# A token tower on one NeuronCore: four value buffers, an early v of batch 4, an early first expert unit, and a new order of the opening

## The reference

```python
h = onehot(x) @ embeddings                          # a row gather
q, k, v = split(layernorm(h) @ w_qkv)               # 16 heads of 16
q = q * cos + rotate_half(q) * sin                  # k too
attn = softmax(q @ k.T * 16 ** -0.5)                # 256 x 256 per head
h = h + (attn @ v) @ w_proj
y = layernorm(h)
chosen = argmax(y @ gate_w.T)                       # one of 8 experts
out = h + y + (y @ expert_w[e].T) * onehot(chosen)  # summed over e
```

## Time and profile before

| | us |
|---|---|
| median of 3 runs (310.54 to 310.95) | 310.89 |
| the profiled execution | 310.0 |
| its span | 308.2 |
| TensorE busy | 283.4 (92%) |
| VectorE busy | 243.4 (79%) |
| ScalarE busy | 132.7 (43%) |
| GpSimd busy | 85.9 (28%) |
| mean granted TensorE clock | 0.983 |

### The profile page before, as it was taken

How to read it: one execution, slowest core, us unless ns; L and a number is a source line. 1 busy time by engine, 2 the same in 40 slices (tenths; PEclk the granted TensorE clock), 3 DMA queues, 4 the chain that set the end, 5 groups by cost and what they waited for, 6 DMA issues and landing times.

```text
span 308.2 us, 5639 instructions
## 1 busy us (share of the span) xinstructions
PE 283.4 (92%) x2063; PEld 203.1 (66%) x2063; DVE 243.4 (79%) x602; ACT 132.7 (43%) x271; POOL 85.9 (28%) x103
## 2 busy tenths in 40 slices
PE   2998799888879999999999999999999999999895
PEld 2775566656646776777767776777666666667674
DVE  8798569968987799887988698878898874656765
ACT  3166117748664534364426433453453444331000
POOL 5736305636265012431222033201200210210300
PEclk9999579999999999999999999999999999999999
DMA  4530410830930580039101940166010010000011
GB/s 117 182 149 17 160 45 6 167 49 14 161 47 5 95 120 2 0 93 147 17 2 36 147 60 2 36 116 94 2 37 1 4 36 2 1 12 26 0 36 34
DMA packets 10803, 17.55 MB, mean 57 GB/s; under 512 B 2024, under 2 KB 4883, under 8 KB 10648
## 3 DMA queue, kind: packets, MB, share of 16 engines
q1 hardware_dynamic: 9988, 16.62, 26.2%
q0 software_dynamic: 768, 0.55, 0.7%
q10 hardware_dynamic: 20, 0.02, 0.0%
HBM read 5.30 MB, written 2.10 MB: 24 GB/s over the span
## 4 chain that ended last, share of the span: by engine, by line
PE 64%; DVE 24%; ACT 5%; issue 3%; DMA 1%; POOL 0%; SPq 0%; DVEq 0%; ACTq 0%
PE e_bank L475 18%; PE f_bank L475 10%; PE o_bank L652 9%; DVE neg_max L1003 7%; PE t_pair L617 5%; DVE acc L1101 4%; PE s_pair L475 4%; PE s_pair L578 3%; PE m_bank L475 3%; PE s_pair L481 2%; PE o_bank L475 2%; PE m_bank L666 2%; PE m_bank L698 2%; ACT probs L867 2%; ACT parts L816 1%
## 5 line engine op out<-in xcount | busy, mean ns | idle before, releaser
L867 ACT ACTIVATE probs<-t_pair 128x512 f32<-128x512 f32 x128 | 69.5, 595 | 80.1 <-PE t_pair L617 79.6
L1003 DVE TENSOR_REDUCE neg_max<-s_pair 128x2 f32<-128x512 f32 x128 | 81.9, 682 | 13.0 <-PE s_pair L578 12.8
L578 PE MATMUL s_pair<-stacks 48*128 48x256 f32 x256 | 49.5, 316 | 1.5 <-DVE neg_max L1003 0.8
L617 PEld LDWEIGHTS t_pair<-stacks 50*128 50x128 f32 x256 | 32.8, 186 | 22.7 <-issue 20.8
L617 PE MATMUL t_pair<-stacks 50*128 50x256 f32 x256 | 46.6, 308 | 1.1 <-DVE neg_max L1003 0.6
L475 PE MATMUL e_bank<-ew_h,y_h 128*128 128x512 f32 x92 | 40.3, 438 | 1.9 <-DVE acc L1101 1.5
L1101 DVE SCALAR_TENSOR_TENSOR acc<-e_bank,mask,acc 128x256 f32<-128x256 f32 x66 | 28.8, 478 | 11.8 <-PE e_bank L475 11.7
L578 PEld LDWEIGHTS s_pair<-stacks 48*128 48x128 f32 x256 | 34.3, 190 | 4.5 <-DVE neg_max L1003 3.5
L475 PE MATMUL e_bank<-ew_l,y_h 128*128 128x512 f32 x92 | 36.4, 396 | 0.0
L394 POOL TENSOR_TENSOR qk<-rope_a,rope_b 128x512 f32<-128x512 f32 x16 | 20.8, 1301 | 56.2 <-DVE rope_b L990 56.2
L475 PE MATMUL e_bank<-ew_h,y_l 128*128 128x512 f32 x92 | 36.2, 394 | 0.0
(11 more groups left out here) (177 smaller groups left out, 542.5 us busy)
## 6 DMA issues: line engine op xcount, KB each, us to landing
stacks<-parts SPq DMA_DIRECT2D x36, 256.0 KB, 6.7
ew_raw<-in_expert_w SPq DMA_DIRECT2D x1, 2048.0 KB, 8.5
out<-res SPq DMA_DIRECT2D x7, 256.0 KB, 2.1
stacks<-parts SPq DMA_DIRECT2D x12, 128.0 KB, 2.8
probs<-in_w_qkv SPq DMA_DIRECT2D x2, 384.0 KB, 3.8
stacks<-max_rows SPq DMA_DIRECT2D x30, 8.0 KB
h<-in_emb,ids POOLq DMA_INDIRECT x16, 2.7
probs<-in_w_proj SPq DMA_DIRECT2D x1, 256.0 KB, 2.7
```

What stands on the lines that cost most here:

```text
L578: m = mm(s_pair[:, half, t * N:(t + 1) * N], stacks[b % STACKS][r:r + KS, pair, 0, t * P:(t + 1) * P], stacks[b % STACKS][r:r + KS, pair, ...
L617: m = mm(t_pair[:, half, c * N:(c + 1) * N], stacks[b % STACKS][r:r + KM, pair, 1, c * P:(c + 1) * P], stacks[b % STACKS][r:r + KM, pair, ...
L867: nc.scalar.activation(probs[:, (2 * v + half) % RING, :, :].rearrange("p c n -> p (c n)"), t_pair[:, half, :], ACT.Exp, scale=SCALE).then ...
L1003: v.tensor_reduce(neg_max[:, k // 4, :, 4 * half + k % 4], s_pair[:, half, :].rearrange("p (t n) -> p t n", t=NT), AX.X, ALU.max, negate=T ...
```

## The change

- Opening: v of batch 0 is projected before visit 2 and v of batch 1 before visit 4; of batch 0's scores those of odd visits go to t_pair, so the transposed scores of step 0 wait for all 16 maxima of batch 0; all of batch 2's qk projection stands ahead of step 0; five fills. Batch 2's x_n is computed by GpSimd (`normed`), not VectorE. The first transpose of maxima writes e_bank.
- Value buffers: four and not three, 17 columns per head and not 32, so `outputs` loads 32 columns that overlap the next head's; the memsets of the padding go, and small ones for the tail come.
- TWO: batch 2's rotate0 and rotate1 go to slots 1 and 3, t0, low0, t1 and low1 one slot later each.
- FOUR: `project_v` of batch 4 goes from slot 5 of step 2 to slot 12 of step 1, into e_bank.
- POST, in every step: the projection from slot 8 to 9, gate from 14 to 15, its transpose from 15 to slot 0 of the next step, `choose` from 15 to slot 1 of the next step and on VectorE ahead of `select`.
- The first expert unit of batch 0 goes from slot 0 of step 2 to slot 15 of step 1.
- `maxima_slot` is 11 always. Fills in step 0: 12 and not 13.

```diff
-VALS = 3
+COLS = 17
+VALS = 4
-        vals = [sb(f"vals{i}", [P, NT, NH, STRIP]) for i in range(VALS)]
+        vals_flat = [sb(f"vals{i}", [P, NT * NH * COLS + STRIP - COLS]) for i in range(VALS)]
+        vals = [f[:, 0:NT * NH * COLS].rearrange("p (t h c) -> p t h c", t=NT, h=NH) for f in vals_flat]
...
-        TWO = dict(rotate0=0, rotate1=1, t0=2, low0=3, t1=4, low1=5, v=7)
-        FOUR = dict(FRONT, stats=-10, norm=-8, x=-7, x_low=-6, qk0=-5, rotate0=-3, qk1=-2)
-        POST = dict(o0=2, o1=4, norm0=3, norm1=5, on=6, o_low=7, proj=8, residual=9, stats=10, g_norm=11,
-                    y=12, y_low=13, gate=14, gate_t=15, choose=15)
+        TWO = dict(rotate0=1, rotate1=3, t0=3, low0=4, t1=5, low1=6, v=7)
+        FOUR = dict(FRONT, stats=-10, norm=-8, x=-7, x_low=-6, qk0=-5, rotate0=-3, qk1=-2, v=-4)
+        POST = dict(o0=2, o1=4, norm0=3, norm1=5, on=6, o_low=7, proj=9, residual=9, stats=10, g_norm=11,
+                    y=12, y_low=13, gate=15, gate_t=16, choose=17)
...
-            return o_bank if k < 2 else f_bank
+            return o_bank if k < 2 else e_bank if k == 4 else f_bank
...
-            return 10 if b < 3 else 11
+            return 11
+        def scores_pair(b, v):
+            return t_pair if b == 0 and v % 2 else s_pair
...
+            def normed(b):
+                pool.wait_ge(f_rstd, b + 1)
+                for t in range(NT):
+                    g.tensor_scalar(xn[:, t, :], h0[:, b * NT + t, :], f_mv[:, t, 0:1], f_rs[:, t:t + 1],
+                                    ALU.subtract, ALU.mult).then_inc(f_normed, 1)
...
             f_rs_of(2)
+            normed(2)
             gather(3)
...
+                if b == 0 and v == 1:
+                    pe.wait_ge(roped, 2 * 2 * NT)
+                if b == 0:
+                    wait(pe, max_ok, 2 * v - 2 - half if v > 1 else 0)
+                else:
+                    wait(pe, max_ok, b * NH + 2 * v - half)
...
+                if v == 0 and b == 0:
+                    pe.wait_ge(max_ok, NH)
...
-                        if b == 0 and s == 0:
-                            project_qk(2, 1, [1])
-                            pe.wait_ge(xl_ok, 3)
                         if b == 0:
-                            fill(m_bank, 3 if s == 0 else 4 if s == 2 else 1)
+                            fill(m_bank, 3 if s < 4 else 1)
...
+                    if b == 1 and s == 15:
+                        experts(0, 0, 0, expert_banks(0))
-                    if here(b, -2) and unit_in(b, s) is not None:
+                    if here(b, -2) and unit_in(b, s) is not None and (b, s) != (2, 0):
                         experts(b - 2, p, unit_in(b, s), expert_banks(b - 2))
...
             visit(-1, 0)
             qk_transpose(1, 0)
+            project_v(0, [0])
             visit(-1, 1)
             qk_transpose(1, 1)
+            project_v(0, [1])
             visit(-1, 2)
+            fill(m_bank, 1)
+            project_v(1, [0])
+            visit(-1, 3)
             x_transpose(2)
-            visit(-1, 3)
-            project_v(0, [0])
+            project_v(1, [1])
+            visit(-1, 4)
             first_max_transpose()
-            visit(-1, 4)
-            project_v(0, [1])
             project_qk(2, 0, [0])
             visit(-1, 5)
-            project_v(1, [0])
             project_qk(2, 0, [1])
+            fill(m_bank, 1)
             visit(-1, 6)
-            project_v(1, [1])
+            project_qk(2, 1, [0])
+            fill(m_bank, 1)
             visit(-1, 7)
-            project_qk(2, 1, [0])
+            project_qk(2, 1, [1])
+            fill(m_bank, 2)
             steps(step)
...
             maximum(0, 0)
             f_norm_a(2)
+            qk_low(1, 0)
             maximum(0, 1)
-            f_norm_b(2)
-            qk_low(1, 0)
+            qk_low(1, 1)
             maximum(0, 2)
-            qk_low(1, 1)
             maximum(0, 3)
```

More of the change, by code:

```diff
@@ L486, in x_transpose @@
                 elif b >= 3:
-                    wait(pe, v_ok, b)
+                    wait(pe, v_ok, 4 if b == 5 else b)
                     wait(pe, qkl_ok, (b - 1) * NT)
@@ L498, in project_v @@
                     pass
+                elif b == 4:
+                    wait(pe, xl_ok, b + 1)
+                    wait(pe, on_ok, NT)
                 elif b >= 2:
@@ L521, in project_qk @@
                 elif b == 2:
-                    wait(pe, qkl_ok, 2)
+                    wait(pe, mt_ok, 1)
                 elif b == 3:
@@ L573, in scores_wait @@
                     wait(pe, stack_in, (b - 2) * 96 + 96)
-                wait(pe, max_ok, b * NH + 2 * v - half)
+                if b == 0 and v == 1:
[4 more added lines that the diff above has]
+                    wait(pe, max_ok, b * NH + 2 * v - half)
             def scores_tile(b, v, half, t):
                 r, pair = place(2 * v + half)
-                m = mm(s_pair[:, half, t * N:(t + 1) * N], stacks[b % STACKS][r:r + KS, pair, 0, t * P:(t + 1) * P],
+                m = mm(scores_pair(b, v)[:, half, t * N:(t + 1) * N], stacks[b % STACKS][r:r + KS, pair, 0, t * P:(t + 1) * P],
                        stacks[b % STACKS][r:r + KS, pair, 1, :], start=True, stop=True)
@@ L583, in first_max_transpose @@
             def first_max_transpose():
-                pe.wait_ge(roped, 2 * 2 * NT)
+                pe.wait_ge(qkl_ok, NT)
                 pe.wait_ge(ml_ok, 1)
                 for t in range(NT):
-                    m = tr(t_bank[1][0:16, N + t * P:N + (t + 1) * P].bitcast(F32R),
+                    m = tr(e_bank[0:16, N + t * P:N + (t + 1) * P].bitcast(F32R),
                            max_parts[:, 0, t, :, :, :].rearrange("p i a j -> p (i a j)"), ident_r[:, :])
@@ L609, in t_scores_wait @@
                     pe.wait_ge(roped, 2 * 2 * NT)
-                    pe.wait_ge(filled, VALS + 1)
+                    pe.wait_ge(filled, 2 * VALS + 1)
                 if v % 4 == 0:
                     wait(pe, m_in[v // 4], b * 32 + 32)
+                if v == 0 and b == 0:
+                    pe.wait_ge(max_ok, NH)
                 wait(pe, exp_ok, b * NH + 2 * v + half - 1)
@@ L714, in experts @@
                     pe.wait_ge(ew_l_ok, 8)
+                    pe.wait_ge(v_ok, 5)
                 if b == NB - 3 and n == 1:
@@ L852, in max_row @@
                 wait(act, mt_ps, b * 2 + u + 1)
-                turned = t_bank[1] if b == 0 and u == 0 else o_bank
+                turned = e_bank if b == 0 and u == 0 else o_bank
                 copy(max_rows[:, u, :], turned[0:16, N:2 * N]).then_inc(mt_ok, 1)
@@ L940, in _ @@
             qk_high(1, 1)
+            values(0)
             qk_high_again(1, 0)
@@ L943, in _ @@
             x_high(2)
+            values(1)
             max_row(0, 0)
-            values(0)
-            values(1)
             steps(step)
@@ L1003, in maximum @@
                     v.tensor_reduce(neg_max[:, k // 4, :, 4 * half + k % 4],
-                                    s_pair[:, half, :].rearrange("p (t n) -> p t n", t=NT), AX.X, ALU.max,
+                                    scores_pair(b, k)[:, half, :].rearrange("p (t n) -> p t n", t=NT), AX.X, ALU.max,
                                     negate=True).then_inc(max_ok, 1)
@@ L1136, in step @@
                         g_norm_b(k)
+                    for k in batches(post, "choose", g_at):
+                        choose(k, k % 2)
                     if here(b, -2) and s > 0 and unit_in(b, s - 1) is not None:
@@ L1161, in step @@
                         y_low(k, k % 2)
-                    for k in batches(post, "choose", g_at):
-                        choose(k, k % 2)
             dve.sem_inc(acc_ok, 1)
@@ L1179, in _ @@
             x_low(0)
-            for i in range(VALS):
-                v.memset(vals[i][:, :, :, HD:STRIP], 0.0).then_inc(h_zero, 1)
             f_norm_b(1)
@@ L1191, in _ @@
             rotate(1, 1)
-            dve.wait_ge(h_zero, NB + VALS)
             for i in range(VALS):
                 v.memset(vals[i][:, :, :, HD:HD + 1], 1.0).then_inc(filled, 1)
+                v.memset(vals_flat[i][:, NT * NH * COLS:], 0.0).then_inc(filled, 1)
             maximum(0, 0)
             f_norm_a(2)
+            qk_low(1, 0)
             maximum(0, 1)
-            f_norm_b(2)
-            qk_low(1, 0)
+            qk_low(1, 1)
             maximum(0, 2)
-            qk_low(1, 1)
             maximum(0, 3)
```

3 lines of the change are left out of this document (2 added, 1 removed).

## The result

| | before | after |
|---|---|---|
| median of the runs made side by side, us | 310.72 (4 runs, 310.23 to 310.95) | 318.75 (4 runs, 316.96 to 319.55) |
| the profiled execution, its span | 310.0, 308.2 | 318.8, 317.0 |
| mean granted clock | 0.983 | 0.982 |

The ratio is 1.0253, 95% interval 1.0207 to 1.0298. The forecast was 312.6 in a range up to 316.3: the sign came right, the size didn't, and the range missed the time.

The account below looks back on a forecast made before the run. TensorE was taken to bound the repeating steps, with recoverable time in the opening. Terms -6.4 + 2.2 - 0.2 + 5.65 + 0.5 = +1.75 on 310.0 gave 311.75, 312.6 as median; range 307.0 to 316.3.

Parts of the forecast that it names:

- opening: Before step 0: the last maximum of batch 0 ends at about 39.7, not 46.1; -6.4 us, bounds -7.2 and -5.0.
- step 0, GpSimd's queue: Step 0: second qk sum behind gathers and weights leaves TensorE 3.6 us idle; net +2.2, bounds 0 and +4.
- step 0, fall of the clock: Step 0: half clock after TensorE's gap; not in the sum, priced at +3.2 us only as a rival.
- rival 1: Step 0: the clock falls behind TensorE's 3.6 us gap; +3.2 us, to 315.8; chance 0.26.
- moved work and gate slots, steps 1 and 2: Steps 1 and 2, with v of batch 4 and first expert unit earlier: net -0.2 us, bounds -1.5 and +1.5.
- the swap from step 2 on: Projection behind outputs(1) delays VectorE's residual: 0.9 in steps 2 to 4, 1.1 in 5 and 6, 0.75 in 7; +5.65.
- the swap in step 1: Step 1: wait for x_n of batch 4 and later residual make visit 6 0.9 us late, inside a net -0.2.
- gate from step 5 on: Start of step 8: no visit between gate and its transpose, so TensorE waits for ScalarE's copy; +0.5 us.
- Rivals 2 and 3: Swap absorbed by VectorE slack, 307.0, chance 0.22; two sides cancel, 310.9 +- 0.6, chance 0.12.
- rival 4: Loads of the packed values are slow: above 317; chance 0.04, shared with another wait.
- Choose was hidden: Repeating step: choose ahead of unit 0's selection hidden with 0.1 us to spare; uncovered, up to 1.0 in five steps.

Follow-up runs that it names:

- fills: The changed kernel with 14 idle matmuls before batch 2's second qk transpose and 6 before batch 4's x transpose; 314.36 us, ratio 1.0133.
- p8: The changed kernel with the projection back in slot 8, all else changed; 308.37 us, ratio 0.9943.
- g3: The changed kernel with GpSimd's gathers of batch 4 and first expert weights in step 0 moved behind the second qk sum; 314.94 us, ratio 1.0152.
- g3p8: The changed kernel with the projection back in slot 8 and step 0's gathers and first expert weights behind the second qk sum; 305.45 us, ratio 0.9847.
- gate14: The changed kernel with gate, its transpose and choose back in slots 14, 15 and 15, choose behind select again; 317.53 us, ratio 1.0220.
- p8late: The changed kernel with the projection back in slot 8, v of batch 4 and the first expert unit back in step 2; 308.78 us, ratio 0.9963.
- open_two: The kernel before with only the change's opening, packed values and fourth buffer, plus batch 2's rotations in slots 1 and 3; 308.8 us, ratio 0.9932.
- b9: The kernel before with one edit, the projection from slot 8 to slot 9; 319.74 us, ratio 1.0281.
- b9not1: The kernel before with the projection in slot 9 for all batches but the first, which stays in slot 8 of step 1; 317.78 us, ratio 1.0241.
- open_gate: The kernel before with only the change's opening, packed values and fourth buffer, plus gate, its transpose and choose in 15, 16, 17; 304.34 us, ratio 0.9798.

## Why the prediction was wrong in size and right in direction

| step of the sum | forecast | measured | from |
|---|---|---|---|
| opening | -6.4 | -5.65 | before and after |
| step 0, GpSimd's queue | +2.2 | +2.2 at full clock | fills |
| step 0, fall of the clock | 0 in the sum (rival 1: +3.2) | +1.5 | fills |
| moved work and gate slots, steps 1 and 2 | -1.1 (the -0.2 without the swap's 0.9) | -1.1 | p8 |
| the swap from step 2 on | +5.65 | +6.35 | p8 |
| the swap in step 1 | +0.9 (within the -0.2) | +4.4 | p8 |
| gate from step 5 on | +0.5 | +1.3 | p8 |
| sum | +1.75 | +8.8 | spans |

The measured terms add to 9.0; spans of different executions, and a fall of the clock that isn't just as long in each, leave 0.2. Two of the recorded figures don't come out of their own working: ten times 0.1 makes the worse bound of the opening -5.4 and not -5.0, and the terms named for steps 1 and 2 give -0.1 and not -0.2. Neither matters for the outcome.

**The opening** went as laid out, and -5.65 lies within the bounds, the worked out -5.4 too. Half of the miss is VectorE's last maximum, 0.4 late; the other half is TensorE's start, 0.36 behind it.

**Step 0.** The order in GpSimd's queue, the gap (3.26 against 3.6) and the net 2.2 were read rightly (visit 5 starts 2.2 late in fills); g3 and g3p8 take the gap and the fall away, though not all of the step's loss. Rival 1, at 0.26, was right that the clock falls and wrong on the price: I took the length of the fall from the one of 10.2 us in the earlier trace rows, and it was 3.4 here and 6.8 once. The ratio it used was good: 0.91 to 1.59 makes 1.46 of a fall of 3.4, and 1.5 was measured (by it 10.2 us would have been 4.4, and not the 3.2 of the text). The Trainium skill, "TensorE: Matmul & The Clock Gate", section "Why this matters for your kernels", warns of idle gaps between bursts of matmuls; this gap of 3.26 and this fall agree. All five profiled kernels that have the gap (3.24 to 3.27 in after, p8, gate14, p8late and open_two) have a fall in step 0, so 0.26 was too little. The opening's fall in before, which rival 1 took for a like case, is like it only in kind: in the ten us before it TensorE's longest wait was 0.48.

**The swap from step 2 on** was the term that I counted against the change, and it holds: 1.06, 1.04, 1.01, 1.20, 1.22 and 0.82 from p8 to after, 6.35 in all, just over the bound of 6.2. b9 and b9not1 show it in a kernel that has nothing else of the change. Rivals 2 and 3 fall with it. The time lies where rival 4 had it, above 317, but not for its reason: sixteen outputs take 1.07 with either layout of the values. That the late residual is what lengthens the steps is read in the rows; that the swap does it is shown.

**The step that failed** is the sentence on step 1: "The wait for o_l (the projection's) turns into a wait for x_n of batch 4 [...]; with VectorE's residual later this makes visit 6 0.9 late", put in a net of -0.2 for steps 1 and 2. The swap's price in step 1 was 0.9 there, and the clock's was nothing. In step 1 the swap costs 4.4: 1.4 at full clock (28.44 in fills against 27.07 in p8), and 3.0 in two falls of the clock. The second failed term is the fall in step 0, left out of the sum: 1.5. The forecast looked for a fall in step 0 alone, where one long gap stood, and not in step 1, where the earlier trace rows already had four gaps and one of them was made longer. With 4.4 in place of 0.9, and with the 1.5, my sum would have been 6.75 and the forecast 317.6; the opening, the swap from step 2 on and the gate make the rest of the 9.0.

**The end and the gate.** The gate's later slot costs 0.35 in step 6 as well, which I didn't price, and 0.8 to 0.9 from step 7 on where I had 0.5. Choose was hidden, as said: steps 3 and 4 of gate14 are as long.

**What stays open.** Why a fall stands behind the 1.40 and the 1.21 us waits of step 1 after, only one in b9 and g3, which have both waits, and none behind the 1.2 us wait of the earlier trace rows in before: no run here separates this. How many falls a kernel has also differs between its executions: the mean clock of the four of after goes from 0.979 to 0.989, and the steps given for it are of one with three falls. Nor is it shown why gate and rotations moved together shorten steps 1 and 2 by 1.4 (p8late) when they give 0.7 and 0.0 alone; in step 2 TensorE waits 0.6 for o_n with the gate alone (open_gate) and not at all with both, and the runs don't say why.

## What to carry to other kernels

When TensorE is full, a swap of two equal pieces is no neutral edit: ask whose input each makes, and give the earlier place to the one that another engine's unbroken chain hangs on. Here some 1 us of delay in each of steps 2 to 7 (6.35 in all) took more than the whole gain of the new opening (5.65), and in step 1 the same delay came with two falls of the clock. When a stretch that already has gaps gets one more wait, add the price of a fallen clock (some 1.5 us a fall here), and check the stretch behind it too. And test a bundle of slot moves one by one on top of its best part: the opening (with the packed values) alone was worth 2.2%, and all other moves together took it away and 2.5% more.

## What the hardware showed that I had not expected

- Falls of the granted clock to its half level lasted 3.4 us (steps 0 and 1 of after), 6.8 (p8late), 10.2 (the opening before) or 13.7 (the opening of b9); one of 3.4 cost some 1.5 us.
- A fall may stand behind small waits: in b9 the clock stayed up behind the 1.39 us wait at 82.9, and fell at 88.7, behind one of 1.21; in the opening of before it fell at 31.8 with no wait over 0.48 in the ten us before. The Trainium skill, "TensorE: Matmul & The Clock Gate", section "Why this matters for your kernels", speaks of idle gaps between bursts; these falls stand behind no gap like the 3.26 of step 0. No run shows that the short waits brought them.
- GpSimd took 1.22 us for one subtract and multiply of 128x256 with two operands per partition, VectorE 0.37 (0.73 for two, at 79.22). The Trainium skill, "GPSIMD Engine Reference", section 4.1, calls operations of one input roughly line-rate; the measurement decides, and it is over three times as long here.
- Loads of 32 columns that overlap the next head's, 17 apart, took no more time than aligned ones: sixteen outputs took 1.07 in b9 (aligned) and 1.07 in after (75.19), both at full clock.
